# GpSimd's split of the turned heads into bf16 parts, in eight pieces of 256 columns instead of three operations of 2048

## The reference, cut to what matters

```python
qkv = x @ Wqkv
q = qkv[..., :2 * Hx].reshape(Bx, 2 * NQ, Sx, HD)        # 32 query heads, HD = 16
k = qkv[..., 2 * Hx:2 * Hx + G].reshape(Bx, NKV, Sx, HD) # 8 key heads
v = qkv[..., 2 * Hx + G:].reshape(Bx, NKV, Sx, HD)
scores = jnp.einsum('bhqd,bhkd->bhqk', q, k) / math.sqrt(HD)
scores = jnp.where(causal, scores, -jnp.inf)
aw = jax.nn.softmax(scores, axis=-1)
aw = aw[:, :, 0] - lam * aw[:, :, 1]                     # pairs of heads
attn = jnp.einsum('bhqk,bhkd->bhqd', aw, v) * (1.0 - LAMBDA_INIT)
```

## Time and profile before

| | us |
|---|---|
| median of 3 runs | 2374.82 (2372.23 to 2375.65) |
| the profiled execution's own time | 2382.39 |
| its span, first to last instruction | 2380.7 |
| PE busy in the span | 2161.4 (91%) |
| DVE busy | 1834.1 (77%) |
| ACT busy | 1582.7 (66%) |
| POOL busy | 594.2 (25%) |
| a group of the attention with a split beside it, start to start (group 2) | 112.4 |
| POOL in L413, L414, L416, 15 of each | 61.2 + 61.3 + 61.1 |

### The profile page before, as it was taken

The page is one execution under the profiler, slowest core; times in us unless marked ns, Lnnn a source line. Parts: engine busy times, 40 slices in busy tenths (PEclk is TensorE's granted clock), DMA queues, the critical chain, the costliest instruction groups (busy, mean ns, idle before and its releaser), DMA issues. The chain is left out here.

```text
span 2380.7 us, 43994 instructions
## 1 busy us (share of the span) xinstructions
PE 2161.4 (91%) x15852; PEld 882.1 (37%) x15852; DVE 1834.1 (77%) x4663; ACT 1582.7 (66%) x3201; POOL 594.2 (25%) x716
## 2 busy tenths in 40 slices
PE   6799999999999999999999999999999889889983
PEld 5132323232332323232323232333222268567831
DVE  3888888888888888888888888888889258334467
ACT  2167777877777777777777778777777735246633
POOL 1213131313223131312221313132211124100067
PEclk8599999999999999999999999999999989899955
DMA  5220302121120202030303031211200020000001
GB/s 156 39 48 6 68 13 61 25 49 33 40 46 27 48 26 48 31 67 6 68 6 68 12 62 23 51 31 43 40 6 2 18 82 0 1 1 1 1 22 49
DMA packets 95985, 84.63 MB, mean 36 GB/s; under 512 B 48544, under 2 KB 81440, under 8 KB 95776
## 3 DMA queue, kind: packets, MB, share of 16 engines
q1 hardware_dynamic: 95776, 81.91, 15.5%
HBM read 26.81 MB, written 16.78 MB: 18 GB/s over the span
## 5 line engine op out<-in xcount | busy, mean ns | idle before, releaser
L726 ACT ACTIVATE probs<-b_bank 128x512 f32<-128x512 f32 (+1 forms) x2304 | 1177.2, 577 | 412.8 <-PE b_bank L879 404.5
L578 DVE TENSOR_REDUCE m_part<-a_bank 128x1 f32<-128x512 f32 x1536 | 970.4, 683 | 120.2 <-PE a_bank L863 114.1
L879 PE MATMUL b_bank<-q_pack,k_pack 64*128 64x512 bf16 (+7 forms) x5120 | 934.1, 352 | 17.4 <-ACT probs L726 14.5
L863 PE MATMUL a_bank<-k_pack,q_pack 64*128 64x512 bf16 (+3 forms) x2560 | 822.3, 361 | 95.9 <-DVE m_part L578 65.2
L911 PE MATMUL acc<-probs,v_tile 128*32 128x512 f32 (+3 forms) x5120 | 600.3, 551 | 3.1 <-POOL probs L437 0.8
L575 DVE CUSTOM_DVE_ANT_0 a_bank<-a_bank,mask_a 128x128 f32<-128x128 f32 (+3 forms) x1024 | 481.0, 515 | 124.8 <-PE a_bank L863 122.3
L879 PEld LDWEIGHTS b_bank<-q_pack,k_pack 64*128 64x128 bf16 (+1 forms) x5120 | 290.2, 95 | 555.3 <-ACT probs L726 426.3
L863 PEld LDWEIGHTS a_bank<-k_pack,q_pack 64*128 64x128 bf16 x2560 | 223.4, 94 | 422.6 <-DVE m_part L578 224.2
L437 POOL TENSOR_SCALAR_AFFINE_SELECT probs<-probs 128x512 f32<-128x512 f32 (+1 forms) x192 | 151.6, 789 | 906.2 <-ACT probs L726 904.2
L911 PEld LDWEIGHTS acc<-probs,v_tile 128*32 128x32 f32 x5120 | 108.4, 108 | 192.1 <-issue 111.3
L575 DVE DVE_READ_ACCUMULATOR2_ANT m_part<- 128x1 f32 x1024 | 144.9, 141 | 0.0
(11 more groups left out here) (191 smaller groups left out, 1824.9 us busy)
## 6 DMA issues: line engine op xcount, KB each, us to landing
q_pack<-part SPq DMA_DIRECT2D x384, 64.0 KB, 2.3
k_pack<-part SPq DMA_DIRECT2D x192, 64.0 KB, 2.3
scratch<-qkv_row SPq DMA_DIRECT2D x16, 512.0 KB, 2.8
heads<-scratch SPq DMA_DIRECT2D x16, 512.0 KB, 3.7
xg<-in_L_attn_x SPq DMA_DIRECT2D x16, 256.0 KB, 2.8
scratch<-qkv_row SPq DMA_DIRECT2D x32, 128.0 KB, 2.7
q_pack<-m_rows SPq DMA_DIRECT2D x256, 2.0 KB
x<-in_L_attn_x SPq DMA_DIRECT2D x4, 1024.0 KB, 11.9
```

Source lines behind the costliest of these rows:

```text
L578: dve.tensor_reduce(out, bank[:, 0:w], AX.X, ALU.max).then_inc(a_maxed, 1)
L726: act.activation(probs[:, n % P_RING, h, at:C], b_bank[bank_no(("B", n, h))][:, at:C], ACT.Exp, scale=HD ** -0.5) \
L863: pe.matmul(a_bank[at % A_RING][:, 0:w], q_pack[buf][rows, hp, 0, q:q + P], k_pack[buf][rows, 0, C * c:C * c + w], start=True, stop=True). ...
L879: ins = pe.matmul(b_bank[bank_no(slot)][:, at:at + C - q], k_pack[par][rows, n2, P * kt:P * (kt + 1)], q_pack[par][rows, h // 2, n2, C * j ...
```

## The change

`split` gets a piece number and a number of pieces, and each of its three operations works on that piece's columns only. In the loop the eight pieces of 256 columns stand at steps 22 to 29 of POOL's list, one per step; the waits for part0 and for the DMAs stand before the first piece, and `parts_ready` rises after the last. A piece has its own wait for its `rest` and `part[1]`. No piece waits for a step: between the pieces POOL has only what its list has there, which is `pair` at step 24. The split before the loop stays in one piece.

```diff
-NORMALISE_AT, DEVIATION_AT, CENTRE_AT, GATHER_AT, SPLIT_AT = 0, 1, 3, 14, 22
+NORMALISE_AT, DEVIATION_AT, CENTRE_AT, GATHER_AT = 0, 1, 3, 14
+PIECES = 8
+SPLIT_AT = range(22, 22 + PIECES)
...
+        def rest_count(n, i):
+
+            return 2 * (n + 1) if n < 2 else 4 + 2 * PIECES * (n - 2) + 2 * (i + 1)
...
-            def split(n):
-
-                pool.wait_ge(part0_ready, upto(n + 1))
-                if not (isinstance(n, int) and n == 0):
-                    pool.wait_ge(packs_in, upto(16 * PACK_DMAS * n))
-                pool.tensor_tensor(rest[0:80, :], headT[0:80, :], part[0][0:80, :], ALU.subtract).then_inc(rest_ready, 1)
-                pool.tensor_tensor(part[1][0:80, :], headT[0:80, :], part[0][0:80, :], ALU.subtract).then_inc(rest_ready, 1)
-                pool.wait_ge(rest_ready, upto(2 * (n + 1)))
-                pool.tensor_tensor(part[2][0:80, :], rest[0:80, :], part[1][0:80, :], ALU.subtract).then_inc(parts_ready, 1)
+            def split(n, i, pieces):
+
+                cols = slice(S // pieces * i, S // pieces * (i + 1))
+                if i == 0:
+                    pool.wait_ge(part0_ready, n + 1)
+                    if n:
+                        pool.wait_ge(packs_in, 16 * PACK_DMAS * n)
+                pool.tensor_tensor(rest[0:80, cols], headT[0:80, cols], part[0][0:80, cols], ALU.subtract).then_inc(rest_ready, 1)
+                pool.tensor_tensor(part[1][0:80, cols], headT[0:80, cols], part[0][0:80, cols], ALU.subtract).then_inc(rest_ready, 1)
+                pool.wait_ge(rest_ready, rest_count(n, i))
+                ins = pool.tensor_tensor(part[2][0:80, cols], rest[0:80, cols], part[1][0:80, cols], ALU.subtract)
+                if i == pieces - 1:
+                    ins.then_inc(parts_ready, 1)
...
-            split(1)
+            split(1, 0, 1)
...
-                    if s == SPLIT_AT:
-                        split(g + 2)
+                    if s in SPLIT_AT:
+                        split(g + 2, s - SPLIT_AT[0], PIECES)
```

## The result

| | before | changed |
|---|---|---|
| median | 2375.24 us (4 runs) | 2335.59 us (4 runs, 2332.7 to 2341.11) |
| ratio, with its 95% interval | 1 | 0.9835 (0.9812 to 0.9858) |
| span of the profiled execution | 2380.7 us | 2333.0 us |
| mean granted clock in it | 0.935 | 0.947 |

The change made the kernel 39.7 us faster by these runs; 42.3 were forecast. Measured twice more beside the kernel before, the changed kernel took 2334.86 us (ratio 0.9796, 0.9782 to 0.9809) and 2335.17 us (0.9816, 0.9793 to 0.9838). Its own time hardly moves; it is the kernel before that lay at 2375.2, 2378.0, 2382.7, 2381.2 and 2380.9 us in the five sets of runs.

What follows compares the result with a forecast made beforehand. DVE's stall behind POOL's split was taken to bound steps 25 to 27, idling PE and dropping its clock. 14 x (3.52 - 0.5) = 42.3 us off 2374.8 gave 2332.5 us, range 2320 to 2352.

Steps and rivals of the forecast that it cites:

- DVE's work on `m_neg` stands until POOL's instruction under way is done: Steps 25 to 27: L590 waits for POOL's split instruction; its loss falls from 2.0 to about 0.3 us.
- The second negation: L595, after L590 and the reduction L578: meets a piece instruction at an unknown place, loss taken as 0.2 us.
- The size of the excess, 3.52 us a group: Steps 25 to 27: 11.73 us with a split against 8.21 without; all but 0.5 us comes back in 14 groups.
- Its two parts, 1.79 us idle and 1.6 us clock: Steps 25 to 27: PE idles 1.79 us before L863, then half clock for 3.20 us costs 1.6; 3.4 in all.
- Rival A: Steps 25 to 27: the stall shrinks but the clock still drops; only 18 us gained, 2357; chance 0.10.
- The clock stays up at the smaller gaps: Steps 25 to 27: with PE's gap at 0.5 us or less, the clock goes from 0.85 to 1.00.
- POOL's pieces: Split in POOL's list: 0.65 us per 256-column instruction, about 2.0 a piece, 16 a split instead of 12.3.
- The cover of `parts_ready`: After the split: POOL's extra 3.7 us cost nothing; 8 us or more remain before its mask; PE, not POOL, releases SP.
- Rivals C and D: C: back-to-back pieces shut DVE out, 2500, chance 0.03. D: L590 stands for something else, no change, 2375, chance 0.03.
- B: Clock drops at steps 19 and 20, in 4 of 14 groups, change in number: 6 us gain to 15 cost.
- The line in the forecast: POOL instruction time by columns: 1.82 ns a column and 0.36 us fixed, giving 0.83 us at 256 columns.

Runs made afterwards that it cites:

- put off: Kernel before, whole split in one piece, POOL waiting for the exponentials of step 26 before it begins: 2334.57 us, ratio 0.9799.
- eight ahead: Changed kernel with all eight pieces of 256 columns placed ahead of `pair`: 2333.57 us, ratio 0.981.
- the reduction: Kernel before, POOL's split unchanged, first negation L590 made as a tensor_reduce with negation from `m_part`: 2346.28 us, ratio 0.9843.

## Why the prediction was right, point by point

- *DVE's work on `m_neg` stands until POOL's instruction under way is done:* right for the two forms that the kernel before has, and shown from three sides: by its place (whole split behind `pair`, or put off), its width (eight, four, two pieces) and its form. The form sets a limit to the sentence: a reduction works on `m_neg` out of SBUF and doesn't wait. Over the thirteen traces (from 60 to 1850 us of the span), 370 negations of the two waiting forms began inside a POOL instruction with 0.1 us or more of it left; each ended within 0.06 us of that instruction's end. The 72 reductions that began so took at most 0.22 us. The second negation, which the forecast gave 0.2 us of loss, lost 0.06; the first 0.28 for 0.3.
- *The size of the excess, 3.52 us a group, to be given back but for 0.5:* right in its sum; 0.35 us stayed, so 3.16 x 14 = 44.2 us against the 42.3 of the forecast.
- *Its two parts, 1.79 us idle and 1.6 us clock:* the split between them was off. This is the one step of the sum that failed, without harm to the sum: PE's longest gap was the wrong measure of the stall. DVE's two losses in the earlier trace rows are 2.00 + 0.19 = 2.19 us, and where the clock holds a stretch is 8.2 us plus these losses, within 0.03 us: 0.34 lost and 8.57 in the change, 0.41 and 8.63 with eight ahead, 0.56 and 8.79 with four, 1.84 and 10.07 with two, 1.32 and 9.55 with the reduction. That leaves 3.52 - 2.19 = 1.3 us for the clock, by subtraction; with two pieces, where it can be measured, most falls cost 1.2 to 1.4. Rival A would have been worth 14 x (2.19 - 0.34) = 26 us, not 18.
- *The clock stays up at the smaller gaps:* right, in all 14 groups, but no row of the kernel before told at what gap it would; this part was argued. The runs give it: the clock fell in none of 14 groups behind 0.15, 0.20 or 0.52 us (the change, eight ahead, four pieces), in 3 behind 1.40, in 11 behind 1.60, in all 14 behind 1.79. The change had room; two pieces would have had none, and there rival A comes near.
- *POOL's pieces:* 0.67 us for the 0.65 taken; `pair` between the second and third, as said.
- *The cover of `parts_ready`:* the conclusion held, a step of it did not. SP's queue by its waits, changed kernel:

```profile
SPq L343 <- PE acc L921: 266.2, 14, 19.0
...
SPq L335 <- POOL part L424: 44.3, 14, 3.6
```

  I had read from the earlier trace rows that POOL doesn't release SP. Now it does, 14 times, for up to 3.6 us: SP is at `pack` long before the group's end and, in the trace, takes the wait for the parts first. It then still waits up to 19.0 us for PE, which is the real cover: about 22 us of waiting as before, only divided.
- *Rivals C and D:* the count above is against both: no negation stood for a second POOL instruction, and each ended with the one that it met. B is seen: the profiles have from 0 to 5 groups with a drop at steps 19 and 20.
- *Against the medians:* the profiles differ by 47.7 us, the first medians by 39.7. The kernel before varies with its clock: its runs have spans from 2368.5 us at a mean clock of 0.942 to 2384.4 at 0.935. Why it was nearer the upper end in the later sets is not settled. That it depends on how the drops fall was argued, not tried, and the later four sets ran on four different chips, a rival that the runs can't tell apart from it.
- *Not in the prediction:* DVE loses time at another place too, near step 14, where POOL orders the heads (the former L426). In group 11 of the changed kernel:

```profile
1374.32 1.25 POOL L436 COPY heads_by_j<-heads 128x1280 f32<-128x1280 f32 x1 [1.69 <-DMA heads<-scratch]
```

```profile
1374.34 1.26 DVE L605 SCALAR_TENSOR_TENSOR m_neg<-m_max,m_neg 128x16 bf16<-128x16 f32 x1
```

  The loss is 1.09 us, and yet this group is as long as those without one, 109.0 us from one first negation of step 25 to the next. PE is busy for 9.84 of the 10 us from 1372 on and waits for DVE nowhere between 1373 and 1380. The change left this place alone, and it costs nothing: a lost microsecond of DVE has a price where it holds up PE, and only there.

## What to carry to other kernels

Look for a small instruction whose mean is several times its median, and lay the two engines' timelines side by side: a wait on another engine's instruction shows as a longer instruction, not as idle time, and no list of waits names it. Three remedies worked here: move the long instruction to where none of the small ones falls, change the form of the small one, or cut the long one into pieces; the first leaves nothing of the stall at that place. First ask whether the engine behind the stall feels it: near step 14 it didn't. Where it does, price the stall by the sum of the delayed instructions' losses on the engine that loses, and add what the clock takes behind PE's gap, which in the kernel before was more than half as much again.

## What the runs showed of the hardware that was not expected

- The granted clock, at one and the same gap of PE (1.60 us, two pieces of 1024), held in 3 groups and fell in 11; behind 1.40 us (the reduction) it held in 11 and fell in 3; at the gaps of 0.15 to 0.52 us left by pieces of 256 and 512 columns it never fell there, behind 1.79 us always. Behind two gaps of 2.83 and 2.99 us (one whole split behind `pair`) it was 0.70 in the mean of group 1's stretch.
- The size of the gap alone doesn't decide: at steps 19 and 20 of the changed kernel PE has the same two gaps, 0.57 and 0.21 us, in group 2, where the clock holds, and in group 3, where it falls to 0.50.
- A POOL instruction of two inputs on 80 partitions took 0.67, 1.16, 2.13 and 4.05 to 4.10 us at 256, 512, 1024 and 2048 columns, or 1.9 ns a column and 0.2 us fixed. The line in the forecast, laid through an instruction of another shape at 512 columns (1.29), had 0.36 us fixed and was too dear.
- Between POOL instructions that follow without a wait DVE always came through. In the whole split behind `pair`, L600 ends at 326.56 and POOL's next instruction is recorded from 326.49; among the 370 cases none stood for two of them in a row.
